# Gate's scores: the gathers wait for the ring of four turns alone, and no longer for pieces of the experts

## What is computed

```
h = (x_flat @ W_gat).reshape(M, HEADS, NUM_EXPERTS)
a_src = (h * att_src).sum(-1)
a_dst = (h * att_dst).sum(-1)
e = leaky_relu(a_src[src] + a_dst[dst], negative_slope=0.2)     # the scores of the edges
... softmax over each node's edges, weighted sum, layernorm, top two of four experts ...
for ei in range(NUM_EXPERTS):
    hh = gelu(x @ W1[ei] + b1[ei])
    out = out + g[..., None] * (hh @ W2[ei] + b2[ei])
```

## Time and profile before

| | us |
|---|---|
| median of 3 runs | 3400.12 |
| lowest, highest | 3395.69, 3422.97 |
| profiled execution | 3410.56 |
| its span | 3408.9 |
| stage of the gate's scores | 2716 to 3215, 499.0 long |

### The profile page before, as it was taken

The page is one execution under the profiler, slowest core; times in us unless marked ns, Lnnn a source line. Parts: engine busy times, 40 slices in busy tenths (PEclk is TensorE's granted clock), DMA queues, the critical chain, the costliest instruction groups (busy, mean ns, idle before and its releaser), DMA issues. The chain is left out here.

```text
span 3408.9 us, 41744 instructions
## 1 busy us (share of the span) xinstructions
PE 2419.1 (71%) x11075; PEld 1584.6 (46%) x11076; DVE 2022.7 (59%) x4071; ACT 1541.4 (45%) x4616; POOL 1634.6 (48%) x1754
## 2 busy tenths in 40 slices
PE   4995667666766566798844577767768788878765
PEld 2553444444444356555422223222227666667654
DVE  4554777777777888400363578888885622222377
ACT  0223767677766244211231578787872122211232
POOL 1544555555553205566673666666622056656300
PEclk8996888888787855699875788898889689988877
DMA  3214555555553013033221333233311211111104
GB/s 96 53 41 133 166 168 172 172 169 160 165 169 105 20 34 99 22 110 102 66 65 39 90 88 88 88 89 91 89 41 16 60 26 32 32 32 26 29 1 174
DMA packets 166205, 291.22 MB, mean 85 GB/s; under 512 B 55996, under 2 KB 100033, under 8 KB 165982
## 3 DMA queue, kind: packets, MB, share of 16 engines
q0 software_dynamic: 79344, 187.14, 19.7%
q1 hardware_dynamic: 74194, 81.65, 7.7%
q10 hardware_dynamic: 12444, 19.77, 1.6%
HBM read 251.13 MB, written 37.30 MB: 85 GB/s over the span
## 5 line engine op out<-in xcount | busy, mean ns | idle before, releaser
L2370 PE MATMUL cv_ps<-cv_msg,cv_hot 128*128 128x512 f32 x880 | 475.8, 694 | 213.9 <-DVE acc L2420 77.6
L950 POOL DMA_INDIRECT at_kv<-kv_tab,e_src x440 | 424.7, 965 | 388.2 <-PE at_a L1097 214.2
L2357 POOL DMA_INDIRECT cv_x<-x_tab,e_src x440 | 425.1, 966 | 237.9 <-issue 107.4
L2794 POOL DMA_INDIRECT gs_h<-h_tab,fc_q x312 | 294.3, 943 | 277.4 <-issue 87.4
L2383 ACT ACTIVATE cv_msg<-cv_x,factors 128x64 f32<-128x64 f32 x1320 | 371.4, 335 | 113.9 <-issue 113.3
L2370 PEld LDWEIGHTS cv_ps<-cv_msg,cv_hot 128*128 128x128 f32 x880 | 185.3, 221 | 504.0 <-issue 290.9
L2420 DVE TENSOR_TENSOR acc<-acc,cv_ps 128x256 f32 x880 | 313.3, 414 | 127.2 <-PE cv_ps L2370 61.8
L2021 POOL DMA_INDIRECT pairs<-gating_pair,gating_place x281 | 275.4, 980 | 213.3 <-issue 70.6
L1097 PE MATMUL at_a<-at_kv,at_hot_e 128*128 128x264 f32 x880 | 271.0, 439 | 53.8 <-ACT at_hot_e L1015 28.3
L2751 ACT ACTIVATE gs_x_hid<-gs_x_h,x_b 128x128 f32<-128x128 f32 x352 | 99.4, 371 | 391.8 <-remote 199.1
L1072 PE MATMUL at_q<-q_parts,at_hot_n 128*128 x1320 | 235.1, 336 | 51.7 <-DVE at_kv L1154 28.0
(11 more groups left out here) (547 smaller groups left out, 4509.3 us busy)
## 6 DMA issues: line engine op xcount, KB each, us to landing
x_space<-in_L_ffn_w SPq DMA_DIRECT2D x16, 1024.0 KB
at_rel_row<-e_rel_rows SPq DMA_DIRECT2D x55, 256.0 KB
experts_out<-gs_y ACTq DMA_DIRECT2D x22, 512.0 KB
x_y<-experts_out SPq DMA_DIRECT2D x22, 512.0 KB, 7.7
at_kv<-kv_tab,e_src POOLq DMA_INDIRECT x440
cv_x<-x_tab,e_src POOLq DMA_INDIRECT x440
kv_tab<-p_qkv SPq DMA_DIRECT2D x25, 256.0 KB
gs_h<-h_tab,fc_q POOLq DMA_INDIRECT x312
```

Source lines behind the costliest of these rows:

```text
L950: nc.gpsimd.indirect_dma_start(out=kv[:, t % (RING * Q4), 0:2 * D], out_offset=None, in_=kv_tab, in_offset=bass.IndirectOffsetOnAxis(ap=e. ...
L2357: nc.gpsimd.indirect_dma_start(out=xg[:, i % RT, u, :], out_offset=None, in_=x_tab, in_offset=bass.IndirectOffsetOnAxis(ap=e.src[:, t:t + ...
L2370: nc.tensor.matmul(ps[u % R][:, :], hot[:, i % 2, u, :], msg[:, i % 2, u, :], start=True, stop=True).then_inc(summed, 1)
L2794: nc.gpsimd.indirect_dma_start(out=hg[:, i % RT, u, :], out_offset=None, in_=h_tab, in_offset=bass.IndirectOffsetOnAxis(ap=e.src[:, i * U ...
```

## The change

Three lines go. POOL's gathers of the gate's scores wait for nothing but `freed`, from turn 4 on.

```diff
                     if i >= RT:
                         pool.wait_ge(freed, i - RT + 1)
                     for u in range(U):
-                        if i and u % 2 == 0:
-                            x = upto(i - 1) + (upto(i) - upto(i - 1)) * u // U
-                            run.passed(pool, x // 8, x % 8)
                         nc.gpsimd.indirect_dma_start(
                             out=hg[:, i % RT, u, :], out_offset=None, in_=h_tab,
                             in_offset=bass.IndirectOffsetOnAxis(ap=e.src[:, i * U + u:i * U + u + 1], axis=0)).then_inc(got[i % RT], 16)
```

## The result

The changed kernel takes 3484.97 us (median of 3 runs, 3479.93 to 3487.92) against 3400.12 before: a ratio of 1.0223, 95% interval 1.017 to 1.0275. It is slower by 85 us; the forecast was 3421 us, and the range ended at 3463.

A forecast was written before the change was run, and what follows sets the result against it. Back-to-back gathers holding PE's hand-overs, with no engine full, were taken to bound the stage: 66 + 34 x 12.3 + 28.5 = 512.7 us against 491.9, +20.8 on 3400.12, giving 3421 us; range 3385 to 3463.

The forecast's parts named there:

- The bound and the mechanism: Gate's scores stage: no engine is full; N back-to-back gathers hold PE's hand-overs, some to 1.43 N us behind the first.
- The "faster" rival: Gate's scores stage: gathers hold nobody and POOL runs ahead, so PE loses 54.2 us of waits: 3346 us, chance 0.07.
- T: Mean time of a turn from `add(1)` to `add(35)`, taken as 12.3 us; each 0.1 us changes the sum by 3.4 us.
- The opening: First gather to `add(1)`: a run of 40 gathers holds to 57.2 us, then turn 0's 9 us of PE work: 66 us.
- bounds 59 to 75: Opening: `add(1)` at 59 us if turn 0 is done inside the hold, 75 if one more turn behind.
- The middle: `add(1)` to `add(35)`: 34 turns, each with a burst of eight gathers set off by `freed`, at 12.3 us each.
- The floor of 8 x 1.43: Middle: no turn is shorter than the hold of its eight gathers, 11.44 us; adds under 11.4 apart would refute it.
- prices near 12.3: Other turn times near the one taken for the middle: the convolution's 11.9 us per eight gathers and before's mean of 12.62.
- The slower rival: Middle: bursts merge into 16 gathers, hold 22.9 us, T = 13.5, +61.6 us: 3462 us; slower by over 1%, chance 0.29.
- The end: `add(35)` to `add(38)`: no gather holds anybody, three turns at PE's pace of 9.5 us, 28.5 us in all.
- What would show it: Signs named for the profile after: run of 40, `add(1)` near 66, runs of eight, adds 12.3 apart, last three about 9.5.
- over 12.7, then bursts merge: Middle: sign that the prediction is wrong, adds over 12.7 us apart, meaning that bursts of gathers merge.

The follow-up runs named there:

- the run with 1.56 us between gathers: Changed kernel with a POOL memset of 128x390 floats ahead of each gather: 3408.58 us (one run), against 3413.51 for the kernel before.
- the kernel of sixteens: Kernel before with one wait in two turns in place of four a turn, so gathers go in sixteens: 3571.91 us, ratio 1.0443 to before.
- the run whose bursts can't merge: Changed kernel with two POOL memsets of 128x1024 between the gathers of one turn and the next: 3439.27 us, ratio 1.0071 to the kernel before.

## Why the prediction was wrong, point by point

**The bound and the mechanism were right for gathers that follow one another closely.** A run of N such gathers holds the others to about 1.43 N us, per gather whatever its rows: the releases read here and in the prediction's rows lie at 1.40 to 1.45 N us for runs of 8, 13, 16, 20, 40, 45 and 80. A release can also come earlier: in one of the five runs of 16 ACT's stands at 21.17 us, 1.32 N. ACT's "remote" wait is that hold. It isn't a price of each gather by itself, as the run with 1.56 us between gathers shows.

The "faster" rival is out: ACT's remote wait grew from 199.1 to 279.9 us and the time with it. The Trainium skill ("SBUF — State Buffer", section "Who interferes with whom") states that PE and ACT never wait on anyone. Beside plain loads from the same queue the trace agrees with that sentence (no remote wait, T = 8.97); beside indirect gathers, read for the whole engine, it doesn't (279.9 us), and the measurement decides. Whether the ports, of which that section speaks, have a part in it no run shows.

**The opening was right, a little high.** Forecast: run of 40, hold to 57.2, `add(1)` at 66, bounds 59 to 75. Measured: run of 40, ACT's last release at 56.37, `add(1)` at 60.06. Four of the five units of turn 0 were done inside the hold, where the forecast had taken it that all were left.

**The middle failed.** T was taken as 12.3 from three runs of eight in the earlier trace rows; it is 14.07, and 34 x 1.77 = 60 us are the whole miss in the stage, less 6 for the opening. The step that failed is the size of this term. Of the 60 us, some 38 lie in the five merged runs of 16, whose ten turns took 16.1 us each, and some 22 in the other 24 turns: the changed kernel's own runs of eight take 13.2 us from start to next start (23 of them, 10.9 to 18.2). The three runs of the earlier trace rows were a mild case. Two of them began right when PE had passed a piece, and the window of that stretch in before shows PE at full clock:

```profile
2941.00:2966.00 25.00, 21.44 (x143) 18.02 (x142) 5.45 (x14) 5.47 (x20) 15.09 (x16) 1.00 0.12 29
```

The mean was 0.90 in before and is 0.85 in the middle after. What PE needs behind a hold was taken as if PE worked through all of it. It works through the first 10 us or so of a run of 16 and hardly at all after. Over the 8.97 us of a turn without holds, the kernels with runs of six (the mean), eight and sixteen lose 3.5, 4.6 and 7.7 us a turn, so the loss grows with the run's length; these kernels differ in their waits as well, and part of the last loss is PE's busy time (above).

The floor of 8 x 1.43 held for the mean alone. Nine of the 34 turns lie under 11.4 us, the shortest at 6.65, each followed by one of 14 us or more. That was the sign named for a hold that is no floor. Five of the nine open the merged runs: an `add` that gets through early sets off the next burst, and the turn after it pays.

**One of the prices near 12.3 was of another kind.** The convolution's 11.9 was called that of a ring with no other wait, but each of its gathers from turn 4 on also waits for ACT (semaphore `scaled`, L2356), which can keep its gathers apart as the pieces did here; no run takes that wait out.

**The slower rival had the mechanism, with too small a price.** It named bursts merging to 16 and took 13.5 from one run of 13 in the earlier trace rows; the ten merged turns here took 16.1 and the kernel of sixteens 16.70. The range ended at that rival's middle value, where it had to reach beyond: its price came from the longest run at hand, of 13, since before's waits kept longer ones from forming. Of the middle's excess over before, 1.56 us a turn, merging makes a third (0.5) by the run whose bursts can't merge, and half (0.8) by the changed kernel's own rows, ten turns at 16.1 instead of 13.2.

**The end was right** (28.5 forecast, 28.74 measured). That all behind `add(38)` would stay the same was not: 7.9 us more, as some 40 of PE's matmuls now lie behind the last add instead of ahead of it (2450 against 2494 from the first gather to it).

**What would show it**: the run of 40, POOL released by `freed` alone, the `add`'s wait for gathers gone, and the last adds 9.1 to 10.3 us apart all came true. ACT's first long idle ended early, at 16.92 us, and it was the later ones that ended at 52.65 and 56.37. "Runs of eight" came true in part (five runs of 16 beside them), "adds 12.3 apart" did not; "over 12.7, then bursts merge" was the sign named in advance. PE's clock did move, and its work a turn rose from 10.3 to 10.4 us: by this the missed term is some 6 us of the stage in PE's busy time.

## What to carry to other kernels

A wait that looks idle, on an engine that is no bound, can be what keeps its transfers apart; before it is taken out, look what the engine does when nothing stops it, and price the longest run that can then form, not the longest that the trace shows. Where indirect gathers run beside dense work, spread them out: here a small memset ahead of each, with the old waits kept, was worth 3% of the kernel. And a price read from the traced cases is a lower bound where the change removes what kept the worse cases from occurring.

## What was not expected of the hardware

Indirect gathers from POOL's queue, 0.94 us of POOL's time each and 1.25 us apart, hold PE, ACT and DVE (longest idle without a visible releaser in the changed kernel: ACT 34.6 us, DVE 13.5) until about 1.43 us for each gather of the run have passed, whether a gather fetches 128 rows or 64; plain loads of the same size from the same queue hold nobody. It is the spacing that decides: at 1.28 us between gathers all of the hold stays, at 1.47 and 1.51 part of it, and at 1.56 nothing. In a long run PE and ACT get an instruction through only now and then: PE one in 0.7 us late in a run of 16 and one in 2.1 us in the run of 40 (2738.67, 2740.78, 2742.88, and then none until 2764.38), ACT one in 1.4 us in the convolution's opening. Which part of the chip the gathers keep to themselves in that time no run shows.
